# Moving the V evacuation to ScalarE and folding the key factor in afterwards, in a fused attention and feed-forward kernel

## The reference

```python
def attn(x, Wq, Wk, Wv, Wo, Wb, bb):          # x is (16, 2048, 1024), H = 16 heads of 64
    q = (x @ Wq).reshape(B, L, H, Dh)
    k = (x @ Wk).reshape(B, L, H, Dh)
    v = (x @ Wv).reshape(B, L, H, Dh)
    beta = sigmoid(x @ Wb + bb)               # one number per token and head
    q = l2norm(q); k = l2norm(k)
    scores = einsum('blhd,bthd->bhlt', q, k)
    scores = scores * beta.transpose(0, 2, 1)[:, :, None, :]
    scores = scores * tril(ones(L, L))        # causal, no softmax
    out = einsum('bhlt,bthe->blhe', scores, v).reshape(B, L, D)
    return out @ Wo

def ffn(x, weights, scale, bias):
    w = (weights >= 0.0) * 2.0 - 1.0
    return clip(einsum('bsi,oi->bso', x, w) * scale + bias, -100, 100)

xn = layernorm(x)
out = x + attn(xn, ...) + ffn(xn, ...)
```

## Time and profile before

| | us |
|---|---|
| time, median of 2 runs | 1082.04 (1081.99 to 1082.08) |
| the profiled execution, its own time | 1082.0 |
| its span on the slowest core | 1079.6 |
| span of the eight cores | 1071.1 to 1079.6 |
| mean granted TensorE clock of the eight cores | 0.949 to 0.953 |

### The profile page before, as it was taken

How to read it: one execution, slowest core, us unless ns; L and a number is a source line. 1 busy time by engine, 2 the same in 40 slices (tenths; PEclk the granted TensorE clock), 3 DMA queues, 4 the chain that set the end, 5 groups by cost and what they waited for, 6 DMA issues and landing times.

```text
span 1079.6 us, 14739 instructions; the slowest of 8 cores (1071.1 to 1079.6 us)
## 1 busy us (share of the span) xinstructions
PE 869.1 (81%) x5320; PEld 386.3 (36%) x5320; DVE 482.5 (45%) x900; ACT 252.4 (23%) x456; POOL 60.3 (6%) x97
## 2 busy tenths in 40 slices
PE   0008764998899979997989879997989978999995
PEld 0004232533344324432444334432444334433442
DVE  1022445533556256624555156525554265622662
ACT  0003222323131311232131311232132313132120
POOL 9100000000000000000000000000000000000000
PEclk9999975899899989999899989999999999999998
DMA  8952012050032301340034101340034102210135
GB/s 159 166 85 79 0 57 80 11 147 1 1 79 59 98 1 40 78 118 1 2 79 99 58 1 40 79 117 1 4 75 94 63 1 51 67 40 1 39 79 117
DMA packets 21125, 63.89 MB, mean 59 GB/s; under 512 B 3648, under 2 KB 3648, under 8 KB 21056
## 3 DMA queue, kind: packets, MB, share of 16 engines
q0 software_dynamic: 11840, 29.40, 16.2%
q1 hardware_dynamic: 9216, 33.56, 8.9%
HBM read 54.60 MB, written 16.78 MB: 66 GB/s over the span
## 4 chain that ended last, share of the span: by engine, by line
PE 71%; DVE 9%; DMA 5%; ACT 5%; issue 4%; POOL 3%; DVEq 1%; ACTq 1%; POOLq 0%
PE pBig L481 21%; PE pBig L781 11%; PE pBig L763 11%; PE pBig L600 8%; PE T L640 5%; DMA scale_pp<-fsc 4%; PE T L712 4%; PE T L502 3%; PE pBig L774 2%; DVE xn_nat L437 2%; DMA outt<-wf 1%; DVE bn L406 1%; DVE bn L410 1%; PE T L694 1%; PE T L449 1%
## 5 line engine op out<-in xcount | busy, mean ns | idle before, releaser
L730 DVE TENSOR_TENSOR sT<-T,mask 128x512 bf16<-128x512 f32 x256 | 164.6, 685 | 134.5 <-PE T L712 134.5
L600 PE MATMUL pBig<-Wv,xnT 128*128 128x512 bf16 x512 | 127.8, 413 | 9.8 <-DVE vt L584 9.8
L763 PE MATMUL pBig<-Wo,ctxT 128*128 128x512 bf16 x512 | 125.4, 389 | 0.0
L781 PE MATMUL pBig<-signT,xnT 128*128 128x512 bf16 x512 | 123.3, 384 | 0.0
L481 PE MATMUL pBig<-xnT,Wq 128*128 128x512 bf16 x512 | 121.3, 380 | 1.4 <-ACT xnT L455 1.4
L481 PE MATMUL pBig<-xnT,Wk 128*128 128x512 bf16 x512 | 120.2, 380 | 0.0
L701 ACT COPY fb<-T 128x512 f32<-128x512 f32 x64 | 37.9, 592 | 235.8 <-PE T L694 229.5
L449 PE MATMUL T<-ident,xn_nat 128*128 128x128 bf16 x256 | 19.4, 235 | 83.0 <-DVE xn_nat L437 81.1
L600 PEld LDWEIGHTS pBig<-Wv,xnT 128*128 128x128 bf16 x512 | 52.3, 105 | 81.6 <-issue 33.3
L807 POOL DMA_DIRECT2D outt<-x x32 | 27.6, 862 | 861.3 <-DVE outt L798 861.3
L494 DVE TENSOR_TENSOR sT<-qT 128x512 bf16<-128x512 bf16 x64 | 27.2, 426 | 106.6 <-ACT qT L489 53.9
(11 more groups left out here) (78 smaller groups left out, 735.0 us busy)
## 6 DMA issues: line engine op xcount, KB each, us to landing
xf<-x SPq DMA_DIRECT2D x32, 512.0 KB, 6.9
outt<-x POOLq DMA_DIRECT2D x32, 512.0 KB, 5.6
out<-outt SPq DMA_DIRECT2D x32, 512.0 KB, 2.6
outt<-wf POOLq DMA_DIRECT2D x8, 512.0 KB, 3.8
Wq<-wq POOLq DMA_DIRECT2D x8, 256.0 KB, 11.7
Wk<-wk POOLq DMA_DIRECT2D x8, 256.0 KB, 23.9
Wv<-wv POOLq DMA_DIRECT2D x8, 256.0 KB, 32.3
Wo<-wo POOLq DMA_DIRECT2D x8, 256.0 KB, 37.0
```

What stands on the lines that cost most here:

```text
L600: (lambda lt, dc, di, pb, sp: lambda e: e.matmul(ps[pb][:, :], sb["xnT"][:, (sp * NT + di) * SPAN + lt * 128: (sp * NT + di) * SPAN + (lt ...
L730: (lambda h01, st_base, gsc=gscs[h01]: lambda e: e.tensor_tensor(sb["sT"][:, (st_base + h01 * 2) * CK:(st_base + h01 * 2 + 2) * CK], ps[gs ...
L763: (lambda cs_, pt, lt, dc, pw: lambda e: e.matmul(ps[pw][:, :], sb["ctxT"][:, (cs_ * (H // 2) + pt) * CK + lt * 128: (cs_ * (H // 2) + pt) ...
L781: (lambda di, dc, span_lt, pyp, sp: lambda e: e.matmul(ps[pyp][:, :], sb["xnT"][:, (sp * NT + di) * SPAN + span_lt * 128: (sp * NT + di) * ...
```

## The change

Job by job, ScalarE now evacuates V with a plain copy from PSUM into `vt`, without the factor. The transposes and copies that make `fkb` no longer stand before job 3; they come after the whole V projection. Behind them VectorE multiplies `vt` by `fkb` in place, eight instructions of 128x512, all operands in SBUF and in bf16. The old `emit_fkb` stays as a function that nobody calls. The chunks are as before.

```diff
-            def emit_fkb():
+            def emit_fkb_unused():
...
             def emit_vevac(lt, dc, pb):
-                P.op("vector",
-                     (lambda lt, dc, pb: lambda e: e.tensor_tensor(
-                         sb["vt"][:, lt * D + dc * 512: lt * D + (dc + 1) * 512]
-                         .rearrange("p (a c) -> p a c", c=DH),
-                         ps[pb][:, :].rearrange("p (a c) -> p a c", c=DH),
-                         sb["fkb"][:, lt * H + dc * 8: lt * H + (dc + 1) * 8]
-                         .unsqueeze(2).broadcast_to([128, 8, DH]), ALU.mult))(lt, dc, pb),
-                     reads=[pb, f"fkb.{lt}"], writes=[f"vt.{lt}.{dc}"], tag=f"vev{lt}.{dc}")
+                P.op("scalar",
+                     (lambda lt, dc, pb: lambda e: e.copy(
+                         sb["vt"][:, lt * D + dc * 512: lt * D + (dc + 1) * 512],
+                         ps[pb][:, :]))(lt, dc, pb),
+                     reads=[pb], writes=[f"vt.{lt}.{dc}"], tag=f"vev{lt}.{dc}")
 
             for i, (lt, dc) in enumerate(vjobs):
-                if i == 3:
-                    emit_fkb()
                 if i >= 3:
                     emit_vevac(*vpend.pop(0))
                 pb = next_big()
...
             for j in vpend:
                 emit_vevac(*j)
+
+            gfk = new_gen()
+            for lt in range(4):
+                P.op("tensor",
+                     (lambda lt, gfk: lambda e: e.transpose(
+                         tv_bf16w(gfk, lt),
+                         sb["fkbT"][:, lt * 128:(lt + 1) * 128],
+                         sb["ident"][0:16, 0:16]))(lt, gfk),
+                     reads=["fkbT", "ident"], writes=[gfk], tag=f"fkT{lt}")
+            for lt in range(4):
+                P.op("scalar",
+                     (lambda lt, gfk: lambda e: e.copy(
+                         sb["fkb"][:, lt * H:(lt + 1) * H],
+                         tv_bf16w(gfk, lt)))(lt, gfk),
+                     reads=[gfk], writes=[f"fkb.{lt}"], tag=f"fkE{lt}")
+            for lt in range(4):
+                for dc in range(2):
+                    P.op("vector",
+                         (lambda lt, dc: lambda e: e.tensor_tensor(
+                             sb["vt"][:, lt * D + dc * 512: lt * D + (dc + 1) * 512]
+                             .rearrange("p (a c) -> p a c", c=DH),
+                             sb["vt"][:, lt * D + dc * 512: lt * D + (dc + 1) * 512]
+                             .rearrange("p (a c) -> p a c", c=DH),
+                             sb["fkb"][:, lt * H + dc * 8: lt * H + (dc + 1) * 8]
+                             .unsqueeze(2).broadcast_to([128, 8, DH]), ALU.mult))(lt, dc),
+                         reads=[f"vt.{lt}.{dc}", f"fkb.{lt}"],
+                         writes=[f"vt.{lt}.{dc}"], tag=f"vfold{lt}.{dc}")
```

## The result

The changed kernel takes 1096.02 us (median of 11 runs), and the kernel before took 1083.58 us beside it (median of 10). The ratio is 1.0121, with a 95% interval of 1.0101 to 1.014: slower by 13 us, which is within 2%. One of the 11 runs took 1134.2 us, with the cores of one die at a lower clock, and doesn't count in the ratio. The forecast was 1085.2 us, 3 us slower. Its profiled execution took 1099.0 us, with a span of 1096.7 us on the slowest core, against 1082.0 and 1079.6 before.

What follows compares the result with a forecast made beforehand. TensorE, busy 81% of the span, was taken as the bound. Terms without the clock summed to +2.5 us, the clock added -7.4 and +8.1, so +3.2 on 1082.0 gave 1085.2 us, range 1063 to 1098.

Steps and rivals of the forecast that it cites:

- Start of job 3: In the V projection job 3 starts 2.91 us sooner in seven spans, -20.4 us, and -1.5 us in the last.
- The chunk's stall: First chunk, spans 2 to 8: context matmul waits for scores behind eight folds, 2.75 us later each, +19.3 us.
- The size of a fold: VectorE's 128x512 fold of V, taken at 689 ns like L584; the bounding rows were 426 and 689 ns.
- this rival: Fast folds: a fold takes 0.43 us, giving 1060.4 us (1053 to 1068); chance 0.15.
- The first span: Sign preparation in the first span starts 5.95 us after the V matmuls end, moving its whole chain by +5.1 us.
- The clock in V (a): In V the idle stretch shrinks from 6.2 to 3.25 us; between 0 and 14.7 us come back, -7.4 taken.
- The clock in the chunk (b): Clock falls behind the chunk's new stall of about 2.6 us; seven spans, bounds 0 and 12.2, two thirds taken, +8.1.
- The rival in which the clock stays up in both places: With slow folds, no clock fall in V or behind the chunk's stall: 1069.8 us; chance 0.10.

Runs made afterwards that it cites:

- e12: The kernel before the change with twenty unused matmuls ahead of the `fkb` transposes in V; 1065.61 us, 0.9848 times before.
- e11: The changed kernel with unused matmuls filling both pauses, thirteen ahead of V's job 3 and eight ahead of the first context group (not in span 1); 1071.02 us.
- e8: The changed kernel with `emit_fkb()` back at job 3 and each fold recorded behind its copy, ScalarE still evacuating; 1083.12 us, 1.0017 times before.
- e1: The changed kernel without the eight folds of each span, so V stays unscaled; 1051.19 us, 0.9663 times before.
- e2: The changed kernel with the dense `mask01` as the folds' second operand in place of the repeated factor (wrong numbers); 1061.75 us, 0.9761 times before.
- e9: The changed kernel with `emit_fkb()` at job 6, behind ScalarE's copy of job 3, and each fold behind its copy; 1056.30 us, 0.9765 times before.
- e4: The changed kernel with `emit_fkb()` at job 6, ahead of ScalarE's copy of job 3, and each fold behind its copy; 1070.00 us, 0.984 times before.
- e7: The kernel before the change with the end of the next span's layer norm moved from ahead of beta to job 7 of V; 1039.20 us, 0.9605 times before.
- e3: The changed kernel with eight unused matmuls ahead of the first context group of each span; 1083.66 us, 0.9947 times before.
- e6: The changed kernel with thirteen unused matmuls ahead of V's job 3 in seven spans; 1076.46 us, 0.9949 times before.

## Why the prediction came out as it did

The time lay inside the range and the verdict within 2% was right; the sum was 10 us short. Against the terms, by the table above:

- **Start of job 3**: -20.4 and -1.5. With the clock held up, V goes from 156.1 (e12) to 136.5 us (e11), -19.6; the changed V includes the four `fkb` transposes behind its last matmul, 0.19 us in each of eight spans, which the prediction counts to the chunk, 1.5 us. So -21.1 against -21.9: right, by the path given. Tanh ended, the copy began at 393.66, job 3 started at 394.36, after 3.10 us idle against 3.25 worked out. e8 shows that the order and not the engine did it.
- **The chunk's stall**: +19.3. e11's chunk is 29.5 us against 26.9, 2.6 x 7 = +18.2, and with the transposes of seven spans counted to it, as there, +19.5. Right. VectorE reached the scores at 410.52, 5.7 us after the V matmuls ended at 394.36 + 10.48 = 404.84 (5.95 worked out), and e1, e2 and e9 show that the folds ahead of them are the reason.
- **The size of a fold**: 689 ns taken, 685 measured. The choice between the two bounding rows was right, and e2 shows that it decided: at 421 ns the kernel takes 1061.75 us, 34 us less than the changed one and close to 2% faster than before, where this rival had 1060.4.
- **The first span**: +5.1, measured 5.4 (44.5 to 49.9 us), but 3.8 between the kernels with the clock held up in V (46.4 to 50.2), so right within what this span's chunk varies. The first L338 started 5.8 us after the V matmuls ended (150.40, against 5.95 worked out). TensorE's wait for the signs grew by 4.0 us in all (21.3 to 25.3), its longest from 3.8 to 6.0.
- **The clock in V (a)**: -7.4 taken, the middle of 0 and -14.7. This step failed. V lost 14.7 us to it before (170.8 - 156.1) and 10.4 after (146.9 - 136.5), -4.3 on the mean of the cores; on the slowest one the V groups give 14.7 and 13.3, -1.4. Half of the pause is gone, but not half of the loss, and the granted clock says why. The prediction read the level as 1.00 while TensorE idles. It was 1.00 up to 392.3 but 0.50 already when job 3 started at 393.8, so part of the lower stretch lay in the pause. After, the level fell once job 3 had begun (0.76 between 394.4 and 395.1, then 0.50), so that all of it fell on matmuls. On the mean of the cores the lower level stood 46.1 us in V before, of which 14.6 lay in pauses and 31.5 on work; after it stood 23.0, with 1.9 in pauses and 21.2 on work. The time at the lower level was halved, the part that costs something fell by a third. Where the level still falls, in 44 of 56, it costs 1.9 us a time against 2.1 before.
- **The clock in the chunk (b)**: +8.1 taken, bounds 0 and 12.2. This was mis-sized as well: 31.1 - 29.5 = 1.6 us in six middle spans and 1.4 in the last make +11.0, and on the slowest core +14.5. The lower level came in 49 of the 56 chunks, more than the two thirds taken, and in three of the slowest core's seven it stood 6.8 us instead of the 3.4 of the earlier trace rows, which the bound of 1.74 us per span left out.
- **The second chunk**: not in the prediction, +4.3 us. That the clock falls there is in the trace of before too, but with the change it is more frequent, 35 of 48 where it was 15. e1 and e9, without the stall, have 260.0 and 260.4 us as before; e4, without it as well, has 267.0, and e11, with it, 261.7. So it isn't explained by the stall alone, and stays open.

The clock terms together were forecast at +0.7 us and came to +10.9 (12.8 before, 23.7 after), which is the whole error: three terms, (a), (b) and the second chunk, each 3 to 4 us off and all the same way. The rival in which the clock stays up in both places was priced at 1069.8, and e11, which forces it, took 1071.02.

## What to carry to other kernels

Moving work off a waiting engine is worth what the next instruction in every queue then waits for: here 20 us of pauses came out of V, and 23 us went in (e12 against e11) because eight folds were put, as a block, between two stages instead of beside the matmuls. Where the tuning question is "which engine evacuates", first ask which instruction stands ahead of the first evacuation in that engine's queue: moving eight instructions of the next span's layer norm was worth 4% (e7), the engine by itself nothing (e8). And cost a pause of TensorE twice, once for its length and once for the matmuls behind it at half clock; halving the pause doesn't halve the second part.

## What the runs showed of the hardware

- A bf16 `tensor_tensor` of 128x512 in SBUF takes 421 ns with two dense operands and 685 ns when one operand repeats each element 64 times (e2 and the changed kernel).
- ScalarE's copy of 128x512 from PSUM to bf16 takes 578 ns, VectorE's multiplying evacuation 689 ns.
- The granted clock fell to 0.50 (1.2 GHz) behind pauses of TensorE of 6.1 us and more in 56 of 56 cases, behind those of 3.1 to 3.5 us in V in 44 of 56, and around the stall of 1.9 us amid small matmuls in 49 of 56. Unused matmuls in the pause keep it at 1.00: 64 to 147 extra matmuls made the changed kernel 12 to 25 us faster (e3, e6, e11), and 140 the kernel before 16 to 18 (e12).
